# Pacing GpSimd's scatters and gathers by the scores of the running step, with four buffers of gathered rows and four of tiles' results

## What is computed

```python
for l in range(2):
    xn = layernorm(x)
    x = x + attention_l(xn) + moe_l(xn)

def attention(xn):            # 16 heads of 16
    q, k, v = (heads(xn @ W.T) for W in (Wq, Wk, Wv))
    p = softmax(causal(q @ k.T / 4))
    return merge(p @ v) @ Wo.T

def moe_0(xn):                # 8 experts, the two best of each token
    w = top2(xn @ W_gate + b_gate)
    return sum(w[e] * (relu(xn @ W1[e] + b1[e]) @ W2[e] + b2[e]) for e in top2)

def moe_1(xn):
    w = top2(softmax(xn @ Wg + bg)); w = w / w.sum()
    return sum(w[e] * (xn @ We[e] + be[e]) for e in top2)
```

## Time and profile before

| | |
|---|---|
| median of 3 runs | 3225.12 us (3223.69 to 3232.07) |
| the profiled execution | 3192.34 us |
| its span | 3190.6 us |
| mean granted TensorE clock | 0.982 |
| busy: TensorE, VectorE, ScalarE, GpSimd | 94%, 74%, 62%, 32% |
| DMA packets | 496.01 MB, 155 GB/s on average |

### The profile page before, as it was taken

One profiled execution on the slowest core, in us unless ns is written; L12 is line 12 of the kernel. 1 busy time (PEld: TensorE's weight loads), 2 busy tenths in 40 slices (PEclk: granted clock), 3 DMA queues, 4 the chain that ended last, 5 costly groups with the idle time before them and its releaser, 6 DMA issues.

```text
span 3190.6 us, 61821 instructions
## 1 busy us (share of the span) xinstructions
PE 3012.9 (94%) x19056; PEld 1580.5 (50%) x19056; DVE 2359.8 (74%) x7245; ACT 1980.9 (62%) x4954; POOL 1025.1 (32%) x1244
## 2 busy tenths in 40 slices
PE   5899999999999999999999999999999999999998
PEld 3454544445455554544445455454545555445443
DVE  5676778777777776878777687777878767677784
ACT  2466666666666666656666666666666666566665
POOL 4115134241522414334151341513324142241512
PEclk8899999999999999999999999999999999999999
DMA  6767455364655635446364554635547364453642
GB/s 188 209 164 215 126 163 156 111 192 118 187 169 153 185 118 171 134 128 182 104 209 142 163 175 124 189 106 159 169 130 212 120 196 148 146 159 99 183 137 77
DMA packets 328101, 496.01 MB, mean 155 GB/s; under 512 B 56832, under 2 KB 242656, under 8 KB 327776
## 3 DMA queue, kind: packets, MB, share of 16 engines
q1 hardware_dynamic: 293536, 416.99, 44.4%
q0 software_dynamic: 24576, 67.14, 6.8%
q10 hardware_dynamic: 9664, 7.93, 0.9%
HBM read 344.19 MB, written 152.84 MB: 156 GB/s over the span
## 4 chain that ended last, share of the span: by engine, by line
PE 80%; DVE 9%; issue 4%; ACT 3%; DMA 1%; SPq 1%; POOL 0%; DVEq 0%; ACTq 0%; another core or an unknown queue 0%; POOLq 0%
PE po L1137 16%; PE pmx L1087 15%; PE pst L1074 14%; PE pst L1121 10%; PE pmx L1207 6%; PE pst L1106 5%; PE pmx L1176 4%; PE pst L1218 4%; PE pst L1095 3%; DVE pmx L836 3%; PE pst L1143 2%; PE pmx L1155 2%; ACT probs L679 1%; DMA xg<-x_slots 1%; DVE x L968 1%
## 5 line engine op out<-in xcount | busy, mean ns | idle before, releaser
L679 ACT ACTIVATE probs<-pst 128x512 f32<-128x512 f32 (+3 forms) x3072 | 1404.6, 496 | 461.6 <-PE pst L1074 431.6
L590 POOL TENSOR_SCALAR_AFFINE_SELECT probs<-probs 128x512 f32<-128x512 f32 x512 | 327.0, 639 | 1800.9 <-ACT probs L679 1798.9
L832 DVE TENSOR_REDUCE rmax<-pmx 128x1 f32<-128x512 f32 x1024 | 668.8, 683 | 140.1 <-PE pmx L1087 131.8
L1074 PE MATMUL pst<-qs,k_first 98*128 98x512 bf16 (+3 forms) x2048 | 692.2, 343 | 34.3 <-issue 18.2
L836 DVE CUSTOM_DVE_ANT_0 pmx<-pmx,mask,rmax 128x128 f32<-128x128 f32 (+3 forms) x1024 | 538.6, 555 | 239.7 <-PE pmx L1087 201.3
L1087 PE MATMUL pmx<-k_first,qs 96*128 96x512 bf16 (+2 forms) x2048 | 669.2, 344 | 21.0 <-DVE rmax L836 6.3
L1137 PE MATMUL po<-probs,v 128*32 128x512 f32 (+3 forms) x6144 | 662.4, 503 | 4.0 <-POOL probs L590 4.0
L836 DVE CUSTOM_DVE_ANT_0 pmx<-pmx,mask 128x128 f32<-128x128 f32 (+3 forms) x1024 | 483.1, 510 | 171.1 <-PE pmx L1087 145.6
L1087 PEld LDWEIGHTS pmx<-k_first,qs 96*128 96x128 bf16 x2048 | 199.2, 98 | 363.9 <-issue 157.7
L1087 PE MATMUL pmx<-k_second,qs 96*128 96x128 bf16 (+3 forms) x1024 | 306.4, 304 | 27.9 <-DVE otok L948 14.1
L1074 PE MATMUL pst<-qs,k_second 98*128 98x512 bf16 (+3 forms) x1024 | 303.7, 303 | 16.4 <-ACT probs L679 9.5
(11 more groups left out here) (121 smaller groups left out, 3349.4 us busy)
## 6 DMA issues: line engine op xcount, KB each, us to landing
wt<-w_tiles SPq DMA_DIRECT2D x161, 513.0 KB
qk_parts<-parts SPq DMA_DIRECT2D x256, 192.0 KB
xg<-x_slots SPq DMA_DIRECT2D x368, 128.0 KB
y_slots<-ys SPq DMA_DIRECT2D x368, 128.0 KB
wt<-w_tiles SPq DMA_DIRECT2D x184, 256.0 KB
qs<-qk_parts SPq DMA_DIRECT2D x128, 192.0 KB
qs<-qk_parts SPq DMA_DIRECT2D x128, 128.0 KB
k_first<-qk_parts SPq DMA_DIRECT2D x64, 192.0 KB, 3.0
```

The source lines that it names most:

```text
L590: pool.affine_select(out=tri, in_=tri, compare_op=ALU.is_ge, fill=0.0, base=0, pattern=[[0, GH], [1, P]], channel_multiplier=-1).then_inc( ...
L679: act.activation(probs[:, u % 2, j, 0:w], ps[:, 0:w], ACT.Exp, scale=DH ** -0.5).then_inc(st_read, 1)
L832: dve.tensor_reduce(rmax0[:, col:col + 1], src, AX_X, ALU.max).then_inc(mx_read, 1)
L1074: pe.matmul(ps[:, 0:w], keys[0:SROWS, j, k % HT * P:(k % HT + 1) * P], qs[0:SROWS, set_no(q, n) % QRING, j, a:a + w], start=True, stop=Tru ...
```

## The change

Three things: `ys` has four buffers and not two, `yk` has four and not eight, and GpSimd, in front of each scatter and each gather whose step belongs to a run's attention, waits until TensorE has written a score of that step: the first score (j = 0) in front of an even a, the third (j = 2) in front of an odd one.

```diff
-XRING, WRING, YRING, GRING = 2, 3, 2, 8
+XRING, WRING, YRING, GRING = 2, 3, 4, 4
...
+            def keep_pace(g, a):
+
+                if unit(g):
+                    pool.wait_ge(st_full, st_done("unit", *unit(g), a % 2 * 2))
+
...
                 for a, q in at_step(g, SCATTER):
+                    keep_pace(g, a)
                     scatter(q, a)
                 for a, q in at_step(g, GATHER):
+                    keep_pace(g, a)
                     gather(q, a)
```

## The result

| | before | after |
|---|---|---|
| median of 5 runs each | 3225.31 us (3223.69 to 3232.95) | 3198.38 us (3188.84 to 3203.12) |
| the profiled execution, its span | 3192.34, 3190.6 | 3198.38, 3196.6 |
| mean granted TensorE clock | 0.982 | 0.982 |

The ratio is 0.9911, with an interval from 0.9892 to 0.993: 0.9% faster, 27 us. Set side by side, though, the two profiled executions say the opposite: after is 6 us longer. The execution of before that the profile shows was 31 us faster than the fastest of its timed runs. So the first thing to settle was where those 31 us lie, since this profile holds little of what the change saves.

A forecast was written before the change was run, and what follows sets the result against it. TensorE, busy 94% of the span, was taken to bound the kernel. Only the VectorE gain counted, all else 0: -6.1 us, 3192.34 to 3186.2, scaled by 1.0% to 3219 us, counted as no change; range 3206 to 3238.

The forecast's parts named there:

- The wait does not hold the scatters back: GpSimd, steps 32 to 35: the new wait for scores is practically met on arrival; cost 0, upper bound 0.3 us each.
- The rival of calmer DMA engines: Steps 35 and 36: paced scatters spread DMA traffic, saving 15 us, scaled 3210, to 3204 with the slow clock; chance 16%.
- The scaling, 3192.34 to 3225.12 as 1.0% of everything: Whole program: timed median 1.0% above the profiled execution, so the forecast 3186.2 us was scaled to 3219.
- Four gather buffers, GpSimd 0.9 us later: Steps 45 to 50: gather a waits for combine a-4, GpSimd runs 0.9 us later; cost 0, range 0 to 2 us.
- 0.4 us of room: Mask of step 50, the tightest: 1.3 us before TensorE needs it, of which 0.9 goes and 0.4 stays.
- VectorE gains 0.47 to 0.94 us in step 48: VectorE's scaling of the maxima (L974) escapes GpSimd's mask and subtraction; 6.1 us gained over fifteen runs.
- the rival in which VectorE is locked out for longer: Step 48: L974 waits for gather 9, mask and subtraction; 13.5 us slower, 3205.8, scaled 3239; chance 17%.
- Four buffers of results: The `ys` buffers, between ScalarE's copy and the stores: they relax a wait no row shows to last; worth 0.
- The end, 0: Last run: its first four gathers wait for scores of steps 42 and 43, before a mask where GpSimd idled; cost 0.
- list of what would show it: Profile after: L974 at 0.2 to 0.5 us, gather 8 0.1 us after combine 4, masks 0.5 to 1 later, scatters unmoved.
- the signs against: L974 or L975 over 1.5 us, TensorE waiting for L595, VectorE for `yk` outside the last run, scatters for scores.
- The DMA share of the window that I named: Steps 35 and 36: a DMA share well under 0.97 would show the forecast wrong.

The follow-up runs named there:

- new profile of before: The kernel before, unchanged, run again for a second profile; that execution took 3226.8 us, and its timed median was 3232.53 us, ratio 1.0005.
- the first group: Kernels timed on one chip against before at 3229.88 us: before unchanged 3232.53, only the waits 3178.08, only the new rings 3241.56, waits before scatters only 3186.72 us.

## Why the prediction was wrong, step by step

- **"The wait does not hold the scatters back", cost 0.** This is the step that failed. I compared the time at which a score is issued with that at which the scatter starts, and took a signal to arrive when its work is done. In step 35 it does not: in after scatter 10 starts 2.40 us after the first score of its step in the mean, 1.56 in the new profile of before. For steps 42 and 43 I did foresee that gathers move by up to 1 us, and put that at nothing because their rows are used late; what it was worth is the late signals of step 43, 1.1 us in each run. The waits alone are worth 1.6% to 1.7% where before takes 3230, and 0.8% where it takes 3202 (there with four `ys`).
- **The rival of calmer DMA engines** had steps 35 and 36 and the scatters right, but not the way: the DMA share of step 35 is 0.96 without scatters 8 to 11 too (seventh run), and nothing is late there. It left out step 43. The slow clock that it counts on is there, as shown above. Its price was too low: half of 2 us in 15 runs, 15 us. In the two profiles of the first group the waits alone save 1.8 + 0.5 us in steps 35 and 36 and 1.1 in step 43, 3.4 x 15 = 51 us against 52 by the medians. Its chance, 16%, rested on the failed step.
- **The scaling, 3192.34 to 3225.12 as 1.0% of everything.** The 33 us lay in two steps, those that the change relieves. A profiled execution that is faster than every timed run should have been taken as a sign that one place differs, not that all are slower.
- **Four gather buffers, GpSimd 0.9 us later.** I began at gather 8, which waits for combine 4. But gather 4 already waits for combine 0, and from there on GpSimd is late; and a gather starts 0.75 us after the combine it waits for, where I let it start 0.1 us after. Gather 8 starts 7.37 us after the first score of step 46 in the mean, 5.54 before, 1.8 us later. The masks of steps 45 to 50 start 0.6 to 2.4 us later, not 0.5 to 1; that of step 50 is the latest. In the seventh run the mask of step 47 starts 2.76 us after the first score of step 48, in the waits alone 1.04. I had left the masks 0.4 us of room; it was gone, and TensorE waits for them as shown above.
- **VectorE gains 0.47 to 0.94 us in step 48.** The term itself came true: L981 no longer has a row above 0.64 us, where L974 had 15 of 1.41. It did so by luck. I had it let through in gather 9; but GpSimd is so late that in 14 of 15 runs L981 lies between gathers 8 and 9 (1472.54 in the rows above) and takes 0.17 to 0.18 us. In the one run in which it meets gather 9 it takes 0.54, and L982 behind it 1.72. And the combines, which I took to stay as they were, lost 50 us of VectorE's time, of which TensorE paid 16 to 21. In place of -6.1 the term is about +16. That is the rival in which VectorE is locked out for longer, in kind (13.5 us forecast), but it hit another instruction, and it was outweighed.
- **Four buffers of results, 0:** right. **The end, 0:** steps of the last run are 1.3 us longer in after, a small miss. That the time lies only 8 us below the range is luck too: a gain of 51 us that was put at 0 and a loss of some 16 that was put at a gain of 6 partly cancel.

So of the list of what would show it, only L981 came out as forecast: gather 8, the masks and the scatters all start later than it says. Of the signs against, the waits of TensorE for L595 and of scatters for scores both appeared, a row of L982 over 1.5 us in one run, while VectorE waits for `yk` hardly more (20.7 us against 16.7). The DMA share of the window that I named was no sign at all: over steps 35 and 36 it is 0.65 in the new profile of before, where the late signals stretch the steps, and 0.73 in after.

## What to carry to other kernels

Where several engines fall idle at once although the work that they wait for has long finished, measure the time from the end of a producer to the start of its idle consumer before believing in any other cause, and see which transfers are in flight there. A wait that is met on paper can still pace a queue, because its own signal can be late as well; here four of them, at the right transfers, did as much as one for each. A ring can be made smaller at no cost until its oldest buffer is wanted before it is free; past that point the delay moves everything behind it on the queue, and what that then meets on the other engines has to be looked up instruction by instruction.

## What was not expected of the hardware

TensorE's signals to VectorE, and in the rows shown to ScalarE and GpSimd too, were late while scatters were under way, those to VectorE by up to 4.9 us (0.04 us is usual), and VectorE, ScalarE and, behind them, TensorE stood still. It takes the indirect DMAs: the stores of step 26 alone delay nothing (0.04 us), and without scatters 8 to 11 step 35 is clean; step 33 keeps 0.6 to 0.9 us in every kernel. It takes more than them, since scatters and gathers in other steps delay nothing, and a full set of DMA engines is not enough (a share of 0.96 without scatters 8 to 11); that the stores are the other half is not shown. By which way the signals are held up no row shows, nor why the same kernel loses 31 us more to it on one occasion than on another; both stay open.
